# Three further matmuls behind the scores of each chunk in a graph attention kernel

## What is computed

```python
def _L1_gnn_ref(x, Wq, Wk, Wv, Wout, edge_index):
    sender, receiver = (edge_index[0], edge_index[1])
    Q = jnp.einsum('nf,hfd->hnd', x, Wq)
    K = jnp.einsum('nf,hfd->hnd', x, Wk)
    V = jnp.einsum('nf,hfd->hnd', x, Wv)
    s = jnp.einsum('hef,hef->eh', Q[:, receiver], K[:, sender]) * scale
    m = jax.ops.segment_max(s, receiver, num_segments=n)
    p = jnp.exp(s - m[receiver])
    denom = jax.ops.segment_sum(p, receiver, num_segments=n)
    alpha = p / denom[receiver]
    msg = alpha.T[:, :, None] * V[:, sender]
    agg = jax.vmap(lambda mh: jax.ops.segment_sum(mh, receiver, num_segments=n))(msg)
    out = jnp.nan_to_num(agg.mean(axis=0))
    return x + out @ Wout
...
x = _layernorm(x + _L1_gnn_ref(x, ...), axis=-1)
```

## Time and profile before

| | |
|---|---|
| median of three runs | 3689.88 us (3683.48 to 3702.83) |
| the profiled execution | 3692.47 us, its span 3690.7 us |
| mean granted TensorE clock | 0.626 of full speed |
| PE busy | 2380.4 us, 64% |
| POOL busy | 1887.0 us, 51% |
| DVE busy | 1742.8 us, 47% |
| ACT busy | 1300.7 us, 35% |

### The profile page before, as it was taken

One profiled execution on the slowest core, in us unless ns is written; L12 is line 12 of the kernel. 1 busy time (PEld: TensorE's weight loads), 2 busy tenths in 40 slices (PEclk: granted clock), 3 DMA queues, 4 the chain that ended last, 5 costly groups with the idle time before them and its releaser, 6 DMA issues.

```text
span 3690.7 us, 75218 instructions
## 1 busy us (share of the span) xinstructions
PE 2380.4 (64%) x18959; PEld 1713.3 (46%) x18960; DVE 1742.8 (47%) x5632; ACT 1300.7 (35%) x3789; POOL 1887.0 (51%) x2340
## 2 busy tenths in 40 slices
PE   3999964666655755576657656655765676666656
PEld 3888853444433533354434434433443454444435
DVE  7999983343333433343334333333432443433337
ACT  3555534333322322233333323322322332333323
POOL 4888874545434544454445445444544454545430
PEclk9999966565555555555555565555555555555557
DMA  4777720111111111111111111111111111111100
GB/s 143 255 253 253 256 62 18 27 30 27 24 27 29 29 22 28 25 31 29 26 24 31 24 28 27 30 23 28 28 23 28 30 27 29 26 31 27 29 14 19
DMA packets 187677, 195.46 MB, mean 53 GB/s; under 512 B 107555, under 2 KB 110451, under 8 KB 185313
## 3 DMA queue, kind: packets, MB, share of 16 engines
q1 hardware_dynamic: 137894, 139.72, 13.3%
q0 software_dynamic: 49280, 50.56, 6.2%
HBM read 184.89 MB, written 5.25 MB: 52 GB/s over the span
## 4 chain that ended last, share of the span: by engine, by line
SPq 43%; issue 37%; DVE 8%; another core or an unknown queue 3%; PE 3%; DVEq 3%; DMA 1%; ACT 1%; POOL 0%; ACTq 0%; POOLq 0%
SPq L453 36%; SPq L451 6%; DVE big L759 2%; DMA visits<-in_src 1%; DVEq L782 1%; PE psM L1485 1%; PE psS L1531 1%; SPq L415 1%; DVEq L805 1%; DVE XS L864 0%; SPq L424 0%; DVE PmPT L785 0%; DVE O L923 0%; PE psVX L1485 0%
## 5 line engine op out<-in xcount | busy, mean ns | idle before, releaser
L622 POOL DMA_INDIRECT XS<-x_dram,dst_bs x1540 | 1461.4, 949 | 1570.8 <-DVE O L923 1020.7
L920 DVE SCALAR_TENSOR_TENSOR l_st<-l_st,alpha,rsum 64x1 f32 x782 | 168.3, 215 | 1468.9 <-remote 824.0
L1250 ACT COPY PmPT<-psT 128x512 f32<-128x512 f32 x196 | 114.7, 585 | 1098.5 <-PE psT L1480 599.4
L1531 PE MATMUL psS<-XT,Ubuf 96*128 96x512 f32 x522 | 490.1, 1040 | 17.2 <-ACT Ubuf L1201 5.5
L1475 PE MATMUL psN<-ident,XS 128*128 128x128 f32 x366 | 112.2, 400 | 587.2 <-issue 404.0
L1485 PE MATMUL psVX<-XS,PmPT 128*128 128x64 f32 x1568 | 333.5, 386 | 215.2 <-ACT PmPT L1250 189.1
L1485 PE MATMUL psM<-XS,dst_bs 128*128 128x64 f32 x1512 | 328.4, 390 | 196.2 <-ACT dst_bs L1250 154.5
L1475 PEld LDWEIGHTS psN<-ident,XS 128*128 128x128 f32 x366 | 78.7, 215 | 802.1 <-issue 802.1
L1485 PEld LDWEIGHTS psVX<-XS,PmPT 128*128 128x128 f32 x1568 | 319.1, 301 | 251.4 <-ACT PmPT L1250 218.1
L1485 PEld LDWEIGHTS psM<-XS,dst_bs 128*128 128x128 f32 x1512 | 312.0, 304 | 233.6 <-ACT dst_bs L1250 177.1
L992 DVE TENSOR_REDUCE rmax<-psS 128x1 f32<-128x512 f32 x391 | 270.3, 691 | 142.4 <-remote 91.3
(11 more groups left out here) (287 smaller groups left out, 4216.6 us busy)
## 6 DMA issues: line engine op xcount, KB each, us to landing
big<-in_edge_attr_2x SPq DMA_DIRECT2D x342, 256.0 KB, 3.2
stat<-x_dram SPq DMA_DIRECT2D x3072, 0.2 KB
big<-dst_turned SPq DMA_DIRECT2D x49, 512.0 KB
XS<-x_dram,dst_bs POOLq DMA_INDIRECT x1540
O<-in_edge_attr_2x SPq DMA_DIRECT2D x48, 256.0 KB, 3.3
O<-codes_dram SPq DMA_DIRECT2D x200, 6.0 KB
x_dram<-x SPq DMA_DIRECT2D x12, 128.0 KB, 2.0
out<-big SPq DMA_DIRECT2D x12, 128.0 KB
```

The costliest lines, as they stand in the source:

```text
L622: pool.indirect_dma_start(xs(k, j), None, x1_dram, bass.IndirectOffsetOnAxis(ap=idx2[b % SB][:, k * CPP + j:k * CPP + j + 1], axis=0)).the ...
L920: dve.scalar_tensor_tensor(out=ls, in0=ls, scalar=al[half], in1=rs[half], op0=ALU.mult, op1=ALU.add)
L1250: act.copy(PTs[a][:, :], psT[:, :]).then_inc(pt_done, 1)
L1531: pe.matmul(psSc[1 - a][:, :], Ubuf[1 - a][:, :], XT[(J - 1) % 3][:, :], start=True, stop=True).then_inc(s_done, 1)
```

## The change

Behind each chunk's scores matmul, PE does three further matmuls. Each has 64 rows of the identity matrix as weights (128 columns) and the first 256 columns of `U` as the moving operand, in float32. They write columns 256 to 511 of the bank `psXc` that the chunk's rows were turned into, and nothing reads them. They wait for nothing of their own and signal nothing. The scores signal `s_done` as before, ahead of them.

```diff
+    WARM, HALF_BANK = 3, 256
...
+            def keep_busy(free):
+                for _ in range(WARM):
+                    pe.matmul(free[:, HALF_BANK:2 * HALF_BANK], ident[0:D, :], U[:, 0:HALF_BANK], start=True, stop=True)
+
             def attend(m, J, i):
...
                     pe.wait_ge(u_done, vv)
                     pe.matmul(psSc[1 - a][:, :], Ubuf[1 - a][:, :], XT[(J - 1) % 3][:, :], start=True, stop=True).then_inc(s_done, 1)
+                    keep_busy(psXc[1 - a])
```

## The result

The changed kernel took 3582.38 us in the median of four runs (3563.37 to 3615.98), the kernel before 3694.31 us (four runs, 3683.48 to 3702.83). The ratio is 0.972, its 95% interval 0.968 to 0.976: faster by 2.8%. The forecast was 3695 us, no change. A ratio leaves out executions more than 1.5% above the fastest of the same kernel, so it can differ from the quotient of two medians.

What follows compares the result with a forecast made beforehand. SP's issue of single-row loads was taken as the bound. 3692.5 + 0 (stage) + 5 (end) = 3697.5, less 2.6 for the profiled execution against the median, gave 3695 us, no change; range 3665 to 3800 us.

Steps and rivals of the forecast that it cites:

- SP's issue sets the stage: SP's queue in attention: issuing 3072 single-row loads takes 3000 us almost without waiting and sets the stage's length.
- rival B: SP's queue: different gather spacing gives more 0.59 us loads, saving about 150 us, 3545 us; chance 0.12.
- 0 (stage): Attention until the last single row: the added matmuls change nothing, SP still ends last and the stage keeps 3000 us.
- rival A: Loop through PE, ACT, DVE and POOL: PE becomes the bound, slower, spread from 3710 to 4086 us; chance 0.18.
- The cost of one matmul: On PE at clock 0.5: 0.85 us for each added matmul, 2.55 us a chunk, bounds 1.7 to 6.2.
- The cover: PE's idle time: 21.6 of 40.8 us per 16 chunks hidden in pairs, 19.2 in the 24.5 us stand for single rows.
- SP's 125 us: SP's mean period for 16 chunks, 3000/24, expected to stay above PE's loop of 119.7 us with the added matmuls.
- The end: Eight chunks after the last single row, where nothing covers the matmuls: +10 us at clock 0.5, taken as +5 us.
- The clock: PE's mean granted clock over attention was expected to rise from 0.57 to 0.7 or 0.8 as gaps fill.
- Rival C: PE at full clock buys nothing in the stage, perhaps some 10 us at the end: 3680 us; forecast with it 0.70.

Runs made afterwards that it cites:

- e18: Kernel before with 16 DMAs of eight neighbouring rows in place of 128 single-row loads in every 16th chunk: 3143.79 us, kernel before 3692.57 us.
- e11: Kernel before with 112 of the 128 single rows loaded as two halves, 240 DMAs: 4872.20 us, kernel before 3712.79 us.
- e16: Kernel before, no added matmuls, POOL's gathers of a chunk waiting for scores of one chunk later: 3567.81 us, ratio 0.970, kernel before 3681.85 us.
- e12: Changed kernel with 112 of the 128 single rows loaded as two halves, 240 DMAs: 4550.58 us, kernel before 3712.79 us.
- e17: Changed kernel with 128 rows instead of 64 and x1 as moving data in the added matmuls: 3695.29 us, ratio 0.994, kernel before 3723.15 us.
- e9: Changed kernel with 128 rows instead of 64 and x1 as moving data in the added matmuls: 2607.68 us, ratio 1.001, kernel before 2605.10 us.
- e1: Kernel before with POOL's wait for scores moved from a chunk's third gather to its first: 2618.84 us, ratio 1.005, kernel before 2608.79 us.
- e4: Changed kernel with 16 DMAs of eight neighbouring rows in place of 128 single-row loads in every 16th chunk: 3008.09 us, ratio 1.143.

## Why the prediction was wrong

**That SP's issue sets the stage** was right for the condition of the trace. e18 takes it away and gets 549 us of the 590 expected; e11 adds to it and pays 0.43 us for every load.

**The step that failed** is in rival B, and the sum rests on it as "0 (stage)": "the number of gathers (1540) and their 1.25 us stay, so SP shares the same time with them, wherever that lies". I took 0.99 us for a load amid gathers and 0.59 us without as two fixed prices. They aren't: by the table of intervals a load costs about 0.5 us when a run of gathers has just begun and 2.8 us after five us of it. The same 1540 gathers took less of SP's time: 2474 us for the loads without the wait, where the sum had 3000 us. Part of that is that the change breaks the runs (117 of eight before, 49 after), part that gathers run while SP waits. For the first part e16 has the gain without added work, e12 with SP as the only bound, and e17 loses it as the long runs come back. B was given a chance of 0.12 and 3545 us; 3582 us is near it, but by luck in part: B's price was 2 quicker loads of 16, and what was measured is a larger saving on SP that PE cuts short.

**What limits the gain** is PE. SP waits 377 us for the update of O; chunks of 7.6 us on PE, without a gap, are the new bound, as the chain says. This is rival A, come in after B. With prompt signals, where SP hides nothing, it decides alone: 15.7%.

**The cost of one matmul** was a little small: 2.86 us for three at the half clock where I took 2.55, within the bounds.

**The cover** was used up, since it rested on SP's 125 us. With SP quicker, PE's waits for single rows fell from 587 us in 24 to 12.3 us in 2, where the prediction had 130 to 400 us left. In e12, where SP stays the bound, the cover holds: PE still waits 901.7 us for single rows, and the kernel is not slower for the added work but 321.6 us faster than e11.

**The end** was put at +5 us and measured +31.8 us: when the last single row is issued, 12 scores matmuls are still to come in the changed kernel and 9 before, and a chunk takes 7.3 us in place of 6.2 us from there. The prediction counted eight chunks and no backlog.

**The clock** was forecast at 0.7 to 0.8 over attention and stayed at 0.59 from 560 to 3400 us (0.57 before). The argument "PE has hardly a gap left" doesn't carry: 15.30 of 15.30 us ran at 0.50. Rival C had the clock of no use to this kernel, and that was right: e9 and e17 raise it to 0.95 and 0.74 and gain 0 and 0.6%.

**What stays open.** Why signals and SP's issue are late amid gathers in some sessions and not in others; no run controls it, and the same chip showed both. Nor is it shown by which path a gather delays them. That shorter runs are the cause of the quicker loads rests on e16 and e17 and on the count of runs. A run in which only the length of the runs is set was not made: a pause of POOL by work of its own after each chunk's gathers would need a wait for the gathers, and was not tried. Against length as the only cause stand the intervals 2 to 4 us into a run, which differ between runs of four and of eight, and in e16 its own runs of four have medians of 1.39 and 1.47 us there. The two interventions also differ in how POOL's breaks lie, and e16 has fewer runs of four than the change for the same gain (there, PE isn't the bound). With late signals neither e1's gate nor one, five or three bfloat16 matmuls were run, nor e4, so how the gain depends on the amount of added work is open.

## What to carry to other kernels

When a queue's issue is the bound, ask what each of its instructions costs next to the others' work and how that changes along a burst, before calling its total fixed: here the same load cost about 0.5 to 2.8 us, while loads added to the queue cost only 0.43 us each. Work added to an engine can pay only by moving something else in time; look for that thing and move it directly. The gate on the gathers gave the same 3% without the 15.7% that the matmuls cost under the other condition (it costs 2.0% there). And measure the kernel before on more than one occasion: 3690 and 2604 us for the same instructions have different bounds, and a change that helps one hurts the other. No version here beats before under both: the gate is faster under one and slower under the other, and 128 rows give 0.994 and 1.001.

## What the runs showed of the hardware that I had not expected

- The same kernel takes 2603 to 2609 us or 3680 to 3725 us, by the session. In the slower case PE's signals reach ACT and DVE only some 4 us late when gathers run long (PE's turning ended at 2020.5 and ACT's copy began at 2024.74), with gathers' transfers no slower.
- Three matmuls of 64 rows went with a mean granted clock of 0.69, three of 128 rows and other data with 0.95, each over attention with prompt signals. PE busy without a gap was granted 0.50 for 81 us and 1.00 for 27 us of one trace.
- Three bfloat16 matmuls a chunk still cost 4.3% with prompt signals; one in float32 cost 7.3%, three 15.7%, five 18.9%. The cost per matmul falls as their number rises, while the mean clock goes from 0.61 (one) over 0.69 (three) to 0.82 (five); without any it is 0.65.
